# Third feed-forward of a four-layer network: routing weights broadcast by DMA through DRAM, gate and up in a ring of three bank pairs

## The reference

```python
logits = jnp.einsum('bsd,de->bse', x, Wg)
top_vals, top_idx = jax.lax.top_k(logits, TOP_K)          # TOP_K = 2
probs = jax.nn.softmax(top_vals, axis=-1)
onehot = jax.nn.one_hot(top_idx, E, dtype=x.dtype)        # E = 8
weights = jnp.einsum('bsk,bske->bse', probs, onehot)
out = jnp.zeros_like(x)
for e in range(E):
    u = jnp.einsum('bsd,dh->bsh', x, W1[e])
    v = jnp.einsum('bsd,dh->bsh', x, W2[e])
    h = u * jax.nn.sigmoid(u) * v
    y = jnp.einsum('bsh,hd->bsd', h, W3[e])
    out = out + y * weights[..., e][..., None]
```

## Time and profile before

| what | value |
|---|---|
| time, median of 3 runs | 1263.78 us (1262.1 to 1264.51) |
| the profiled execution's own time | 1262.16 us |
| its span in the trace | 1260.3 us |
| TensorE busy | 85% of the span |
| VectorE, ScalarE, GpSimd busy | 50%, 41%, 14% |
| mean granted clock of TensorE | 0.929 |

### The profile page before, as it was taken

How to read it: one execution, slowest core, us unless ns; L and a number is a source line. 1 busy time by engine, 2 the same in 40 slices (tenths; PEclk the granted TensorE clock), 3 DMA queues, 4 the chain that set the end, 5 groups by cost and what they waited for, 6 DMA issues and landing times.

```text
span 1260.3 us, 12073 instructions
## 1 busy us (share of the span) xinstructions
PE 1066.9 (85%) x3752; PEld 460.1 (37%) x3752; DVE 633.9 (50%) x1123; ACT 518.1 (41%) x960; POOL 182.4 (14%) x160
## 2 busy tenths in 40 slices
PE   4898989898899999998847958677778999997677
PEld 2354545444222222222514633222224444442333
DVE  3213131332888778641513434799964555552443
ACT  4322222323367767675303435655552222226510
POOL 9000000000000000000173530366620000000000
PEclk9899999998799999998788979799997999999779
DMA  9600000020021212113013420000000000000001
GB/s 191 214 2 0 0 0 0 0 59 23 20 64 39 64 40 64 39 46 91 11 31 89 135 77 0 1 0 1 0 1 0 1 1 0 0 0 0 1 0 33
DMA packets 60307, 42.13 MB, mean 33 GB/s; under 512 B 17352, under 2 KB 57277, under 8 KB 60164
## 3 DMA queue, kind: packets, MB, share of 16 engines
q1 hardware_dynamic: 57956, 38.80, 11.3%
q0 software_dynamic: 2304, 2.76, 0.7%
HBM read 29.59 MB, written 13.67 MB: 34 GB/s over the span
## 4 chain that ended last, share of the span: by engine, by line
PE 61%; DVE 14%; issue 13%; ACT 8%; SPq 2%; DMA 1%; POOL 1%; DVEq 0%; ACTq 0%; POOLq 0%; another core or an unknown queue 0%
PE psum L566 59%; ACT sb_scr L1256 5%; DVE sb_scr L1736 3%; DVE sb_scr L1986 2%; DVE sb_scr L1995 2%; ACT psum L1256 1%; DVE sb_small L1697 1%; PE psum L1028 1%; SPq L347 1%; PE psum L1010 1%; DVE sb_x L1617 0%; DVE sb_h L1600 0%; ACT L1256 0%; DVE sb_scr L1638 0%; DVE sb_scr L1810 0%
## 5 line engine op out<-in xcount | busy, mean ns | idle before, releaser
L1256 ACT ACTIVATE sb_scr<-psum 128x512 f32<-128x512 f32 (+2 forms) x648 | 323.1, 537 | 491.9 <-PE psum L566 386.7
L566 PE MATMUL psum<-sb_h,sb_wide 128*128 (+1 forms) x448 | 226.4, 612 | 0.0
L1736 DVE TENSOR_REDUCE sb_scr<-psum 128x2 f32<-128x1024 f32 x128 | 154.3, 1223 | 43.7 <-PE psum L566 43.1
L566 PE MATMUL psum<-sb_scr,sb_wide 128*128 128x512 f32 x256 | 132.2, 598 | 6.1 <-DVE sb_scr L2057 6.1
L566 PEld LDWEIGHTS psum<-sb_h,sb_wide 128*128 128x128 f32 x448 | 86.0, 196 | 99.4 <-issue 99.0
L534 POOL DMA_INDIRECT expert_in<-sb_scr x32 | 31.2, 975 | 586.1 <-DVE sb_scr L1881 576.7
L1680 DVE TENSOR_SCALAR sb_scr<-psum,sb_b 128x512 f32<-128x512 f32 x48 | 36.0, 751 | 152.9 <-PE psum L566 152.9
L566 PE MATMUL psum<-sb_kstack,sb_qstack 96*128 96x512 bf16 x256 | 100.9, 406 | 6.4 <-DVE sb_scr L1736 6.0
L1256 ACT ACTIVATE sb_scr<-psum,sb_b 128x512 f32<-128x512 f32 x60 | 40.8, 687 | 159.2 <-PE psum L566 159.2
L566 PE MATMUL psum<-sb_qstack,sb_kstack 128*128 128x512 bf16 x256 | 99.1, 392 | 3.5 <-ACT sb_scr L1256 2.0
L566 PE MATMUL psum<-sb_wparts,sb_pick 96*128 96x512 bf16 (+1 forms) x192 | 66.4, 402 | 39.0 <-DVE sb_scr L1995 28.8
(11 more groups left out here) (222 smaller groups left out, 1299.8 us busy)
## 6 DMA issues: line engine op xcount, KB each, us to landing
sb_qstack<-q_bounce SPq DMA_DIRECT2D x48, 96.0 KB
sb_kstack<-k_bounce SPq DMA_DIRECT2D x144, 32.0 KB
expert_in<-sb_scr SPq DMA_DIRECT2D x4, 645.0 KB, 7.2
sb_scr<-expert_in SPq DMA_DIRECT2D x8, 322.5 KB
expert_out<-sb_scr SPq DMA_DIRECT2D x4, 512.0 KB, 5.9
sb_wide<-L_ffn_W SPq DMA_DIRECT2D x2, 1024.0 KB, 7.4
sb_scr<-expert_out SPq DMA_DIRECT2D x8, 256.0 KB, 4.7
q_bounce<-sb_scr SPq DMA_DIRECT2D x12, 128.0 KB, 2.4
```

Source lines behind the costliest of these rows:

```text
L566: return nc.tensor.matmul(out_, w, r, start=start, stop=stop, **kw)
L1256: return nc.scalar.activation(out_, in_, func, **kw)
L1736: v.reduce_max(headmax[:, g % 2, t:t + 2, j], banks, AX.X).then_inc(sem("maxed"), 1)
```

## The change

The routing weights are no longer cut into parts and no longer spread by TensorE. TensorE transposes `weight2` as fp32, a batch at a time, into bank 6 (`turn_weights2`), ScalarE copies the 8 rows to `turned2`, SyncE stores them in DRAM (`weight_rows2`, 8 rows of 2 KB for a batch), waits for the store, and loads each row back to all 128 partitions: 32 broadcasts of 256 KB to `spread2`, a ring of eight. VectorE's second product reads the weights there.

Gate and up have three pairs of banks (0 to 5) instead of two. The products of gate and up are kept in a ring of eight (`prod2`), the hidden tiles in a ring of three (`hid2`). All 64 steps of the four batches are written out as one sequence n. TensorE does `up2(n)`, after n = 4 to 7 the turn of one batch, and from n = 8 on `down2(n - 8)`. VectorE makes product n and then hidden tile n - 6. The sums of the batches alternate between banks 7 and 6, and the add to `x` follows ten steps after the batch's last step. VectorE takes the difference of the two best scores right after the maxima, ahead of the search for indices, and puts products 0 and 1 in between the steps of the routing. The fourth feed-forward's instructions stay as they are; the counts of its semaphores are adapted.

```diff
+        UP2, PROD2, HID2, SPREAD2, HID_LAG, DOWN_LAG = 3, 8, 3, 8, 6, 8
@@ SyncE, after its last loads
+            for n in range(NB * E2):
+                b, e = divmod(n, E2)
+                if e == 0:
+                    sp.wait_ge(sem("turned2_ready"), b + 1)
+                    sp.dma_start(weight_rows2[b], turned2[0:E2, b, :]).then_inc(sem("rows2_stored"), 16)
+                    sp.wait_ge(sem("rows2_stored"), 16 * (b + 1))
+                if n >= SPREAD2:
+                    sp.wait_ge(sem("hid2_ready"), 2 * (n - SPREAD2) + 2)
+                sp.dma_start(spread2[:, n % SPREAD2, :], weight_rows2[b, e:e + 1, :].broadcast_to([P, S])).then_inc(spread2_loaded[n % SPREAD2][0], 16)
@@ TensorE
-            for i in range(2):
-                up2(0, i)
-            turn_weights(1, 4)
...
-                        mm(bank(4 + e % 2), pick[:, e, :], wparts[:, b, :]).then_inc(sem("weights_spread"), 1)
...
-            experts2(0, True)
-            with pe.Fori(1, NB) as b:
-                experts2(b, False)
-            down2(NB - 1, NC - 1)
+            def up2(n):
+                b, i = divmod(n, NC2)
+                e, k = divmod(i, 2)
+                if n >= UP2:
+                    pe.wait_ge(sem("prod2_ready"), n - UP2 + 1)
+                s0 = 2 * (n % UP2)
...
+            def turn_weights2(b):
+                if b == 0:
+                    pe.wait_ge(sem("route_weights"), 1)
+                else:
+                    pe.wait_ge(sem("turned2_ready"), b)
+                for t in range(TT):
+                    m = nc.tensor.transpose(psum[0:E2, 6, t * P:(t + 1) * P], weight2[:, b * TT + t, :], eye[:])
+                m.then_inc(sem("weights_turned2"), 1)
+            def down2(n):
+                b, i = divmod(n, NC2)
+                e, k = divmod(i, 2)
+                pe.wait_ge(sem("hid2_ready"), n + 1)
+                if i == 0 and b == 1:
+                    pe.wait_ge(sem("turned2_ready"), NB)
+                if i == 0 and b >= 2:
+                    pe.wait_ge(x_ready, x_before(FFN2) + b - 1)
+                mm(bank(7 - b % 2), w3_2[:, e, k, :], hid2[:, n % HID2, :], i == 0, i == NC2 - 1).then_inc(sem("down2_done"), 1)
+            for n in range(N2 + DOWN_LAG):
+                if n < N2:
+                    up2(n)
+                if 4 <= n < 4 + NB:
+                    turn_weights2(n - 4)
+                if n >= DOWN_LAG:
+                    down2(n - DOWN_LAG)
@@ ScalarE
-            copy_parts(1, 4)
+            for n in range(N2):
+                act.wait_ge(sem("up2_done"), n + 1)
+                if n >= UP2:
+                    act.wait_ge(sem("prod2_ready"), n - UP2 + 1)
+                f(gact2[:, n % UP2, :], bank(2 * (n % UP2)), ACT.Silu).then_inc(sem("gact2_ready"), 1)
+                if 4 <= n < 4 + NB:
+                    copy_weights2(n - 4)
@@ VectorE
-            v.memset(weight_parts, 0.0).then_inc(setup, 1)
...
+            def hidden2(n):
+                at = n // 2
+                loaded, before_ = spread2_loaded[at % SPREAD2]
+                dve.wait_ge(loaded, before_ + 16 * (at // SPREAD2 + 1))
+                dve.wait_ge(sem("prod2_ready"), n + 1)
+                if n >= HID2:
+                    dve.wait_ge(sem("down2_done"), n - HID2 + 1)
+                v.tensor_tensor(hid2[:, n % HID2, :], spread2[:, at % SPREAD2, :], prod2[:, n % PROD2, :], ALU.mult).then_inc(sem("hid2_ready"), 1)
...
+            best_values(st, scores2)
             v.tensor_tensor(peak1, top1[:, :, 1], top1[:, :, 0], ALU.subtract).then_inc(setup, 1)
+            two_best(st, scores2, E2)
+            product2(0)
...
+            product2(1)
...
-            st.then(lambda: v.tensor_copy(weight_parts[:, :, 0:E2], weight2))
-            st.then(lambda: v.tensor_tensor(weight_rem, weight2, weight_parts[:, :, 0:E2], ALU.subtract))
-            st.then(lambda: v.tensor_copy(weight_parts[:, :, 32:32 + E2], weight_rem))
...
+            v.tensor_tensor(weight2, first1[:, :, 0:E2], second1[:, :, 0:E2], ALU.add).then_inc(sem("route_weights"), 1)
+            for n in range(2, N2 + HID_LAG):
+                if n < N2:
+                    product2(n)
+                if n >= HID_LAG:
+                    hidden2(n - HID_LAG)
+                if n >= NC2 + HID_LAG + 4 and (n - HID_LAG - 4) % NC2 == 0:
+                    add_batch2((n - HID_LAG - 4) // NC2 - 1)
+            add_batch2(NB - 1)
```

More of the change, by code:

```diff
@@ L216, in build @@
         inverse = view(9344, S)
-        gact0 = view(0, 2 * S).rearrange("p (r s) -> p r s", r=2)
-        prod0 = view(2048, 2 * S).rearrange("p (r s) -> p r s", r=2)
-        hid0 = view(4096, 2 * S).rearrange("p (r s) -> p r s", r=2)
+        UP2, PROD2, HID2, SPREAD2, HID_LAG, DOWN_LAG = 3, 8, 3, 8, 6, 8
+        gact2, hid2, turned2, prod2, spread2 = (view(at, n * S).rearrange("p (r s) -> p r s", r=n)
+                                                for at, n in ((0, UP2), (1536, HID2), (3072, NB), (6656, PROD2), (10752, SPREAD2)))
+        NC2, N2 = 2 * E2, NB * 2 * E2
         def by_expert(at):
@@ L283, in build @@
                                             (("gathered", NB), ("x_loaded", 2), ("y_stored", 2)))
+        weight_rows2 = nc.dram_tensor("weight_rows2", [NB, E2, S], F32, kind="Internal").ap()
+        spread2_loaded = [(group, NB * (STACKS if group in stacked else 16 * PARTS)) for group in stacked + max_stacked]
         ATTN0, FFN0, ATTN1, FFN1, ATTN2, FFN2, ATTN3, FFN3 = range(8)
@@ L1158, in _ @@
-            turn_weights(1, 4)
-            def down2(b, i):
-                e, k = divmod(i, 2)
[L1162 to L1177, removed]
-                        mm(bank(4 + e % 2), pick[:, e, :], wparts[:, b, :]).then_inc(sem("weights_spread"), 1)
[L1179 to L1185, removed]
@@ L1523, in _, with copy_weights2 @@
             f(sum1, peak1, ACT.Exp).then_inc(sem("act_setup"), 1)
-            copy_parts(1, 4)
[L1525 to L1532, removed]
+            def copy_weights2(b):
+                act.wait_ge(sem("weights_turned2"), b + 1)
+                f(turned2[0:E2, b, :], psum[0:E2, 6, :], ACT.Copy).then_inc(sem("turned2_ready"), 1)
+            for n in range(N2):
[5 more added lines that the diff above has]
+                    copy_weights2(n - 4)
             layer_norm(ATTN3)
@@ L1558, in _ @@
             layer_norm(FFN3)
-            copy_parts(2, 1)
+            copy_parts(1, 1)
             for b in range(NB):
@@ L1808, in two_best @@
                 st.wait()
+            def two_best(st, scores, n):
                 for t in range(NT):
@@ L1839, in _ @@
             st.wait()
+            best_values(st, prob1)
             two_best(st, prob1, E1)
@@ L2019, in _, with product2, add_batch2 @@
             layer_norm(FFN2)
[L2020 to L2023 removed]
+            def product2(n):
+                dve.wait_ge(sem("gact2_ready"), n + 1)
+                if n >= PROD2:
+                    dve.wait_ge(sem("hid2_ready"), n - PROD2 + 1)
+                v.tensor_tensor(prod2[:, n % PROD2, :], bank(2 * (n % UP2) + 1), gact2[:, n % UP2, :], ALU.mult).then_inc(sem("prod2_ready"), 1)
+            def hidden2(n):
[6 more added lines that the diff above has]
+                v.tensor_tensor(hid2[:, n % HID2, :], spread2[:, at % SPREAD2, :], prod2[:, n % PROD2, :], ALU.mult).then_inc(sem("hid2_ready"), 1)
+            def add_batch2(b):
+                dve.wait_ge(sem("down2_done"), b * NC2 + NC2)
+                add_to_x(b, 7 - b % 2)
             dve.wait_ge(sem("route_scored"), 2)
             st = Steps("q_step", 0, R2_STEPS, Q_STEPS + R1_STEPS)
[L2026 removed]
+            scores2 = psum[:, 6, 0:NT * E2].rearrange("p (t e) -> p t e", t=NT)
+            best_values(st, scores2)
             v.tensor_tensor(peak1, top1[:, :, 1], top1[:, :, 0], ALU.subtract).then_inc(setup, 1)
+            two_best(st, scores2, E2)
+            product2(0)
             dve.wait_ge(sem("act_setup"), 3)
@@ L2035, in _ @@
                 st.did(v.tensor_tensor(one_hot[:, :, 0:E2], one_hot[:, :, 0:E2], each(pair_weight[:, k, :], E2), ALU.mult))
-            st.then(lambda: v.tensor_tensor(weight2, first1[:, :, 0:E2], second1[:, :, 0:E2], ALU.add))
-            dve.wait_ge(setup, SETUP.index("parts2") + 1)
-            st.then(lambda: v.tensor_copy(weight_parts[:, :, 0:E2], weight2))
-            st.then(lambda: v.tensor_tensor(weight_rem, weight2, weight_parts[:, :, 0:E2], ALU.subtract))
-            st.then(lambda: v.tensor_copy(weight_parts[:, :, 32:32 + E2], weight_rem))
             st.wait()
             st.end()
[L2044 to L2059, removed]
+            v.tensor_tensor(weight2, first1[:, :, 0:E2], second1[:, :, 0:E2], ALU.add).then_inc(sem("route_weights"), 1)
[7 more added lines that the diff above has]
+            add_batch2(NB - 1)
             layer_norm(ATTN3)
```

18 lines of the change are left out of this document (8 added, 10 removed).

## The result

The changed kernel takes 1242.58 us (median of 4 runs, 1239.49 to 1246.64), the kernel before 1263.49 (4 runs); the ratio is 0.9835, 95% interval 0.9809 to 0.9861. The forecast was 1244.4. On another chip it was 1235.25 (5 runs) against 1257.2 (9 runs), ratio 0.9827 [0.9814, 0.9841]. So the gain was 20.9 and 22.0 us where 19.4 were forecast.

A forecast was written before the change was run, and what follows sets the result against it. TensorE, busy 85% of the span, was taken as the bound; 21.2 us removed less 1.7 for turns gave 19.4, so 1263.78 - 19.4 = 1244.4 us. Range 1242 to 1247, to 1251 with late weights, low clock and reloads.

The forecast's parts named there:

- The sum: Third feed-forward on TensorE: 21.2 us removed less 1.7 us added, 19.4 us gained, last end at 1120.4.
- Hole and low clock: Stage start: TensorE's 7.69 us wait for the routing goes, and 2.5 us from six instructions at the low level.
- the clock would stay up from 956.2: First pairs: granted clock stays 1.00 as work continues; rival, low until 970.2, 6.4 us lost, 1250.8 us, 5%.
- Spreads: Steady part: 31 TensorE products that spread the routing weights, 0.22 us each, go: 6.8 us.
- Borders: Between batches: three TensorE losses of 0.73 us go, through two banks for the add and a written-out stage: 2.2 us.
- Tail: Stage end: TensorE's wait before the last weighted product goes, covered by the last nine weighted products: 1.5 us.
- Turns: Added TensorE work in the stage: 16 transposes of fp32 weights, costing 1.7 us (bounds 1.1 and 2.0).
- The DMA path at nothing: Stage start: store 2.4 us and broadcast 3.0 finish before TensorE's first weighted product at 971.2, so no cost.
- The slack: Stage start: first hidden tile ready at 970.4, 0.7 us before TensorE wants it.
- No wait recurs for a broadcast: Sign on VectorE in the stage: prediction is wrong if its waits for broadcasts recur for every expert.
- the slower case: Rival, 4%: broadcasts bound the stage; slower than before from 5.3 us each, 1301 us at 6.5.
- none at the four copies: Rival on ScalarE, 3%: each of four copies costs two table loads, 3.5 us lost, 1247.9 us.

The follow-up runs named there:

- without the lead: Changed kernel with two pairs of banks, all four turns behind the second pair and each weighted product after the next pair: 1245.83 us against 1256.22 before.
- six-pair lead: Changed kernel with weighted products six pairs behind gate and up instead of eight, hidden tiles four instead of six: 1245.49 us against 1259.59 before.

## Why the prediction was right

**The sum.** From 957.41 I had the last weighted product end at 1120.4; the next product starts at 1120.68 behind it. The stage's gain was 19.05 us for 19.4. The mechanism is the one forecast, term by term. Some of the closeness is luck: the clock rose at 955.7 instead of 956.3, which gave 0.3 us and made up for the wait of 0.3 us.

**Hole and low clock, 10.2 us.** Shown by putting them back (10.39, for a hole of 8.8 us instead of 7.7 and a low level that ended sooner behind it). That the clock would stay up from 956.2 held.

**Spreads, 6.8.** Shown by putting them back: 6.94.

**Borders, 2.2.** Gone in the trace. That the order removes them and not the written-out loop is shown by the loops written out in the kernel before; there my expectation of a loop overhead failed. So of the prediction's two reasons for this term, the two banks and later add and the writing out, only the first holds.

**Tail, 1.5.** Down to one wait of 0.29 us; back at 1.33 without the lead.

**Turns, 1.7.** Four took 0.44 us each.

**The DMA path at nothing.** I had the first hidden tile at 970.4 and the product at 971.2; they came at 969.1 and 970.76. The store took 1.5 us instead of 2.4, the broadcast 3.5 instead of 3.0, and copies came 0.6 sooner. The slack was 1.66 us and not 0.7. The Trainium skill (DMA: Bandwidth & Descriptors, Anatomy of one DMA) gives its fit, 2.0 us plus bytes over 436 GB/s, for DMAs that GpSimd issues; these were SyncE's. The estimate by it was 4.6 us for both, and this trace has 1.48 + 3.50 = 4.98, nearer to that than to my 5.4. Part of this is luck: the estimates by the fit are 2.0 for the store and 2.6 for the broadcast, one too long and one too short, as were my 2.4 and 3.0. The six-pair lead shows what lies beyond the slack.

**The rivals.** No wait recurs for a broadcast, and the broadcasts moved at up to 339 GB/s in a stretch of 2 us, so the slower case had no place. From the first pair to the last ScalarE had one table load, at 953.23, and none at the four copies.

**What the sum did not have** is the 1.5 to 2.6 us by which the medians gained more. In both traces of the changed kernel the part behind the stage took 117.0 us, in that of the kernel before and of its written-out form 120.3 and 120.4. But variants of the changed kernel, whose instructions there are the same, had 117.0 to 121.9. Whether the changed kernel meets fewer dips by its position in time, or by chance, is open: no run fixes where the dips fall. So this part of the gain is not explained.

## What to carry to other kernels

Where one engine works without gaps, price a change by the instructions that it takes from or gives to that engine, and by the idle stretches that it closes, each with the low clock that follows it in the trace. A slow path (here 5 us through DRAM) costs next to nothing if enough independent work stands ahead of it; the needed lead can be counted in pairs from the trace, and buffers in SBUF carried it here, not more PSUM banks. When two versions differ by a few us, compare the length of the changed stage in the traces as well as the medians.

## What the runs showed of the hardware

In one trace the granted clock fell to the low level for 3.4 us behind 32 products of 8 columns issued without a gap; in three traces, with a pair of full products between two blocks of 16, it did not. It did not fall in a wait of 1.89 us amid dense work; in a hole of 8.8 us, with one turn behind 2.14 us of idle time, it fell. The same 235 TensorE instructions behind the stage took from 117.0 to 121.9 us in thirteen traces, with mean granted clocks of 0.85 to 0.82:

```profile
1118.06:1240.00 121.94, 89.95 (x235) 40.63 (x233) 48.90 (x117) 41.47 (x67) 0.00 (x0) 0.82 0.03 9
```

That row is of the kernel with two pairs of banks. Broadcasting one row of 2 KB to 128 partitions took about as long as a plain load of the size: the first of eight was in use 3.5 us after its issue, where the first of the eight plain loads of the earlier trace rows landed after 3.0 us and the slowest after 5.4, and 267 GB/s moved in the two microseconds around its landing.

ScalarE's hardware loop over Silu loaded a table at the head of every pass (1.28 us each); the same loop written out loaded it once.
